# Router sum and conv low part trade places on VectorE inside the adjacency loop of a fused GNN and FFN kernel

## The reference

```python
# per batch, x normalised over its features
x_conv = relu(conv17(relu(bn(conv1(x)))) + x)          # 1-D convolution over nodes
s      = x @ w_se.T + b_se                             # 3-dimensional embedding
A      = exp(-dist(s, s)) * adj                        # 1024 x 1024
x_nmp  = A @ relu(x @ w_msg.T + b_msg)
x      = x + gru(concat(x_conv, x_nmp), x)
# FFN: the upper half of the nodes by router weight
weights = layernorm(x) @ wr + br                       # one number per node
sel     = x[top_k(weights, 512)[:511]]
x[sel] += gelu(sel @ w1 + b1) @ w2 + b2, times its weight
```

## Time and profile before

| | |
|---|---|
| median of three runs | 583.39 us (582.86 to 583.49) |
| the profiled execution, its own time | 582.93 us |
| its span | 581.1 us |
| mean granted clock of TensorE | 0.983 |
| busy: TensorE, VectorE, ScalarE, GpSimd | 92%, 83%, 60%, 48% of the span |

### The profile page before, as it was taken

One profiled execution on the slowest core, in us unless ns is written; L12 is line 12 of the kernel. 1 busy time (PEld: TensorE's weight loads), 2 busy tenths in 40 slices (PEclk: granted clock), 3 DMA queues, 4 the chain that ended last, 5 costly groups with the idle time before them and its releaser, 6 DMA issues. The chain is left out here.

```text
span 581.1 us, 8982 instructions
## 1 busy us (share of the span) xinstructions
PE 537.1 (92%) x2928; PEld 412.4 (71%) x2928; DVE 481.0 (83%) x1060; ACT 350.3 (60%) x607; POOL 278.9 (48%) x360
## 2 busy tenths in 40 slices
PE   2799999999999999999999999999999989799960
PEld 2696689668966897689768976798679857566630
DVE  5896569689998999899989999899889987979320
ACT  3655666765676577648674857585748463564430
POOL 3522243523358235824582447344724462467773
PEclk9799999999999999999999999999999999999995
DMA  8440510072007400650056002700180017122210
GB/s 276 185 147 2 218 72 2 0 269 94 2 1 229 171 2 1 194 206 1 1 155 243 1 2 76 288 1 1 57 306 1 0 52 237 41 75 71 77 60 27
DMA packets 34381, 55.84 MB, mean 96 GB/s; under 512 B 2322, under 2 KB 23845, under 8 KB 34208
## 3 DMA queue, kind: packets, MB, share of 16 engines
q1 hardware_dynamic: 30240, 48.95, 24.4%
q0 software_dynamic: 4096, 6.33, 3.2%
HBM read 44.74 MB, written 14.75 MB: 102 GB/s over the span
## 5 line engine op out<-in xcount | busy, mean ns | idle before, releaser
L767 ACT ACTIVATE tr<-D 128x512 f32<-128x512 f32 x128 | 76.2, 596 | 78.6 <-PE D L1441 76.7
L1441 PE MATMUL D<-V,U 128*128 128x512 f32 x128 | 89.3, 698 | 0.5 <-DMA adjb<-in_adj 0.5
L1447 PEld LDWEIGHTS M<-cst,adjb 128*128 128x128 f32 x512 | 63.8, 141 | 35.2 <-issue 22.0
L1447 PE MATMUL M<-cst,adjb 128*128 128x128 f32 x512 | 76.8, 272 | 0.3 <-DVE tz L1093 0.3
L563 POOL DMA_INDIRECT sel<-R,ridx x64 | 64.8, 1012 | 20.1 <-issue 17.0
L1470 PE MATMUL N<-tz,msgF 128*128 128x512 f32 x128 | 64.2, 593 | 0.0
L1470 PE MATMUL N<-ga,msgF 128*128 128x512 f32 x128 | 64.2, 593 | 0.0
L1325 PE MATMUL C<-zR,wc 128*128 128x256 f32 x208 | 60.6, 291 | 0.0
L1326 PE MATMUL C<-zR,wc 128*128 128x256 f32 x208 | 58.7, 282 | 0.0
L1327 PE MATMUL C<-zR,wc 128*128 128x256 f32 x208 | 58.7, 282 | 0.0
L1123 DVE TENSOR_SCALAR_CACHE_REDUCE junk<-W,R 128x1024 bf16<-128x1024 f32 (+3 forms) x64 | 51.7, 808 | 5.8 <-ACT W L729 5.8
(11 more groups left out here) (232 smaller groups left out, 1509.9 us busy)
## 6 DMA issues: line engine op xcount, KB each, us to landing
adjb<-in_adj SPq DMA_DIRECT2D x7, 4096.0 KB, 14.1
adjb<-sel SPq DMA_DIRECT2D x8, 516.0 KB, 4.8
out<-R SPq DMA_DIRECT2D x8, 512.0 KB, 3.4
xall<-in_x SPq DMA_DIRECT2D x7, 512.0 KB, 5.5
adjb<-in_adj SPq DMA_DIRECT2D x1, 3072.0 KB, 16.9
R<-in_conv_w SPq DMA_DIRECT2D x1, 1088.0 KB, 7.8
adjb<-in_adj SPq DMA_DIRECT2D x1, 1024.0 KB, 4.9
sel<-R,ridx POOLq DMA_INDIRECT x64
```

Of the source, the lines that this page charges most:

```text
L767: nc.scalar.activation(E[:, u % NE, :], Db[u % NH][:, :], ACT.Exp, scale=-1.0).then_inc(exp_ok, 1)
L1441: MM(Db[h][:, :], U[:, t * P:(t + 1) * P], V[:, half(h)], start=True, stop=True).then_inc(d_ps, 1)
L1447: i = TR(Mb[h][:, k * P:(k + 1) * P], adjb[:, h * TH + k, t * P:(t + 1) * P], ident)
```

## The change

In each batch's adjacency loop on VectorE, `conv_lo(b, 1)` goes from step 11 to step 12, and `node_weights(b - 1, ...)` from step 12 to step 11; in the last batch `node_weights` goes from step 11 to step 10. No operation is added or removed, and no other engine's stream is touched.

```diff
@@ -1196,14 +1196,14 @@
                         conv_sum(b, 1)
                     if u == 6:
                         conv_lo(b, 0)
-                    if u == 11:
+                    if u == 12:
                         conv_lo(b, 1)
                     if b > 1 and not (last and u < 6):
                         if u in AHEAD_AT:
                             rank_tiles_ahead(b - 2, q, AHEAD_AT[u])
                         if u in BEHIND_AT:
                             rank_tiles_behind(b - 2, q, BEHIND_AT[u])
-                    if not first and u == 12 - last:
+                    if not first and u == 11 - last:
                         node_weights(b - 1, 1 - q)
                     if u == 13 and b > 1:
                         indices(b - 2, q, 1)
```

## The result

The changed kernel takes 579.06 us (median of four runs, 578.95 to 579.67) against 583.43 us for the kernel before (582.86 to 583.49). The ratio is 0.9929, with an interval of 0.9912 to 0.9947: 4.4 us less, between 3.1 and 5.1. The forecast was 580.6 us with a range of 579.5 to 582.3.

The account below looks back on a forecast made before the run. TensorE was taken as the pacing engine, losing 5.00 us at row transposes waiting for the router sum. Gains of 0.57 (batch 2), 1.84 (batches 3 to 6) and 0.36 (batch 7) made 2.77 us: 583.39 to 580.6 us, range 579.5 to 582.3.

Parts of the forecast that it names:

- The wait on `w_ok`: TensorE's row transposes waiting for the router sum; claimed gone whole, 0.74 us in batch 2, 0.63 in batches 3 to 6.
- `conv_lo` one step later: VectorE's adjacency loop; claimed to cost nothing, since the gates read it behind the loop, with at least 1.8 us of cover.
- foretold 3.58: VectorE's time from the start of `weigh(11)` to that of `weigh(13)`, claimed to stay 3.58 us as before.
- the second rival: Line 1107's small operation blocks `weigh(12)` during the DMA issue: 583.9 us, or 582.2 if half held; chance 0.12.
- The lead of each batch passes on: Between batches; claimed each gain is kept, as VectorE's 1.56 us and GpSimd's 5.02 us of waiting exceed 0.57 us.
- the third: Rival: the lead is given back within the batch to a VectorE or GpSimd wait, about 583.0 us; chance 0.05.
- the last rival: The row transposes were not held by the sum, so nothing is won and new waits remain: 585.6 us; chance 0.04.
- From the end of such a product to the released load the trace shows 0.17 us: Release time from a `weigh` product to TensorE's transpose load, read in batch 7; claimed as new wait in batches 2 to 6.
- 5 x 0.17 = 0.85 us of loss: New waits of TensorE's adjacency transposes for the later `weigh(12)`, 0.17 us in each of batches 2 to 6.
- batch 7 as 1.38 us of new wait in full: Transposes of tile 13 wait for a later `weigh(11)`; 1.74 us of loss replaced by 1.38, gain 0.36 us.
- The first rival: The whole wait goes without a new one in batches 2 to 6: 3.62 us gained, 579.8 us; chance 0.08.
- Line 1107 should end with the DMA issue beside it: Sign in the changed profile: `node_weights`' small second operation on VectorE is held until GpSimd's DMA issue ends.

Follow-up runs that it names:

- The sum alone: Only `node_weights` one step earlier, `conv_lo` left at step 11, against the kernel before: 603.11 us for 604.64 on chip 8, ratio 0.9983; 0.9986 on chip 6.
- the filler: Kernel before plus four small GpSimd additions ahead of each batch's third indirect DMA: ratio 0.9994 on chip 1; 594.53 us for 604.61 on chip 6.

## Why the prediction was wrong

**Right.** The wait on `w_ok` went whole. `conv_lo` one step later cost TensorE nothing on the first chip. `weigh(13)` starts 178.72 - 175.13 = 3.59 us behind `weigh(11)`, foretold 3.58. The small operation did not hold up `weigh(12)`, which starts 0.14 us behind its start, so the second rival fell. The lead of each batch passes on: 3.90 us of steps become 3.93 us at the last distance matmul, so the third fell too. The sum alone and the change show that the row transposes did wait for the sum, which settles the last rival.

**Wrong: "From the end of such a product to the released load the trace shows 0.17 us".** This is the step that failed. The load at 475.23 in the earlier trace rows names `weigh(11)` as its releaser, but it wasn't waiting: its idle time is the usual 0.24 us, the same as in the earlier trace rows with no releaser, and so 0.17 us was a distance between two events that had nothing to do with each other. Real releases measure 177.85 - 177.79 = 0.06 us in batch 2 and 473.20 - 473.15 = 0.05 us in batch 7. The new wait of batches 2 to 6 is 0.02 us at the load and nothing in the step. The term 5 x 0.17 = 0.85 us of loss should have been nought.

**Wrong in size: batch 7 as 1.38 us of new wait in full.** The step grew by 3.49 - 2.40 = 1.09 us. Some of the difference is the release time again, the rest is in how a wait at a load reaches the step. The load idled 1.50 us, 1.26 more than its usual 0.24, but the matmul queue idled only 0.88 us, and behind the wait the loads follow one another faster: the row loads start 473.59 - 473.20 = 0.39 us behind, against 178.39 - 177.85 = 0.54 us in batch 2. The sum alone showed the same in batch 2: 1.04 us more at the load, 0.88 us in the step. So batch 7 gained 0.65 us, not 0.36.

With these two, the sum is 3.25 + 0.65 = 3.90 us in place of 2.77, which is 579.5 us. The first rival, with 0.08, had the right mechanism (a quicker release) and came to 3.62 us with the old value of batch 7. The lower end of the range was built on that rival, so it left no room for a quicker release and a cheaper batch 7 together; at its upper end the spread of 0.3 us is added as 0.1 (582.2 + 0.3 would be 582.5), which decided nothing. The medians differ by 4.4 us with an interval of 3.1 to 5.1. The 0.5 us above 3.90 fit the two groups of executions at different granted clocks, like against like 3.9 us, and no repeat of the change on a chip of the first kind tests it.

**Not foreseen: what `conv_lo` does to GpSimd.** The prediction counted what moved past VectorE's queue and stopped there. In its new place `conv_lo` (177.71 to 178.81) overlaps the issue that starts at 178.08, and that takes 1.58 us instead of 0.97. In its old place it started 0.50 us behind the start of an issue, and that issue took 1.25 us with it (175.20, before) and 1.25 us without it (175.23, after). The Trainium skill (SBUF — State Buffer, section Who interferes with whom) says that a VectorE instruction with two SBUF inputs contends with a GpSimd instruction that reads SBUF. The trace agrees, with 0.61 us, if the issue is taken as such an instruction (it takes its indices from `ridx` in SBUF). Of a VectorE instruction in a two-port mode the same page says that whoever issues first has the ports for the whole instruction and the other blocks fully. Taken for line 1107, as the prediction did, the measurement differs and decides: started 0.19 us into an issue at 176.78, and 0.35 us into one in batches 3 to 6, it takes its plain 0.24 us. Before, started 0.50 us into one, and 0.60 us in batches 3 to 6, it lasted until the issue's end. That "Line 1107 should end with the DMA issue beside it" was therefore wrong as well.

On the first chip this shift is free. On three others (8, 6 and 12) the change is worth 15.7 to 17.8 us, of which the router wait is 3.9, and the stretches behind batches 2 to 6 are 34.9 us with it. The kernel before, profiled on chip 0, has there a wait of ScalarE that costs 2.2 us or more in each. That it goes by the time at which the DMAs are issued is shown, by two edits on GpSimd alone (half of the DMAs later, and the filler). What holds the signal of the recorded transposes (the copy starts 2.8 us later than it does with half of the DMAs moved), and why some chips show it and others don't, stays open: the trace names no releaser.

## What to carry to other kernels

A releaser's name in the trace does not make a wait: compare the idle time with the one that the same instruction has when nothing can hold it, and take release times only from places where it is clearly longer. A wait at a weight load is not the loss of the step; the loads and matmuls behind it close up, and about 0.2 us of 1.3 came back here. When a two-input VectorE operation is moved, look at which DMA issue on GpSimd it now meets, and measure on more than one chip before the gain is given a cause.

## What the runs showed of the hardware

- The same kernel takes 583.6 us on chip 1 and 604 to 612 us on chips 0, 6, 8 and 12. The extra time stands in five waits of 3.5 us, which lengthen the stretches around them by 12.5 us and shrink to 0.75 us when GpSimd's DMAs are issued 0.6 us later (filler, 604.6 to 594.5 us), and in a tail about 9 us longer (110.0 against 100.6 us on chip 0), whose cause stays open.
- A 128x512 operation with two SBUF inputs, 1.1 us long, lengthened an indirect DMA issue from 0.97 to 1.58 us when the issue started 0.37 us into it, and to 1.75 us when it started 0.19 us into it. An issue that had started 0.50 us ahead of the operation kept its 1.25 us. A 128x8 operation beside such an issue took 0.24 us when it started 0.19 to 0.35 us into it, and lasted until the issue's end (0.47 and 0.38 us) when it started 0.50 and 0.60 us into it.
- From the end of a VectorE product to the start of the released weight load: 0.05 to 0.06 us.
- The same idle time of TensorE, 2.15 us, was followed by full clock in one execution and by 3.4 us at 1.2 GHz in another; the second lost 1.55 us on TensorE and 0.7 us in its span.
